# Another bound for half of the query weight and a new order of the opening, in a cross-attention and quantised feed-forward kernel on Trainium2

## What is computed

```python
def xattn(q, ctx, Wq, Wkv, Wout):           # 16 heads of 64; 1024 queries, 64 keys for each batch
    qp = q @ Wq.T                           # Wq 1024 x 1024
    k, v = split(ctx @ Wkv.T, 2)            # Wkv 2048 x 256
    scores = einsum(qh, kh) / sqrt(64)      # masked: query row i sees keys 0..i
    return (softmax(scores) @ vh) @ Wout.T  # Wout 1024 x 1024

def ffn(x, W):                              # per-tensor e4m3 quantisation of x and W
    return ((quant(x) @ quant(W).T) * (sx * sw)).astype(bfloat16)

x = x + xattn(layernorm(x), ctx, Wq, Wkv, Wout)
return x + ffn(layernorm(x), W)
```

## Time and profile before

| | before |
|---|---|
| median of 3 runs (lowest, highest) | 1737.17 us (1736.21, 1738.05) |
| profiled execution | 1736.76 us |
| its span, first to last instruction | 1734.8 us |
| TensorE busy | 1706.3 us (98%) |
| VectorE busy | 1337.4 us (77%) |
| ScalarE busy | 672.6 us (39%) |
| GpSimd busy | 182.7 us (11%) |
| mean granted TensorE clock | 0.999 of full speed |

### The profile page before, as it was taken

How to read it: one execution, slowest core, us unless ns; L and a number is a source line. 1 busy time by engine, 2 the same in 40 slices (tenths; PEclk the granted TensorE clock), 3 DMA queues, 4 the chain that set the end, 5 groups by cost and what they waited for, 6 DMA issues and landing times.

```text
span 1734.8 us, 27825 instructions
## 1 busy us (share of the span) xinstructions
PE 1706.3 (98%) x11485; PEld 810.6 (47%) x11513; DVE 1337.4 (77%) x1910; ACT 672.6 (39%) x638; POOL 182.7 (11%) x142
## 2 busy tenths in 40 slices
PE   7999999999999999999999999999999999999998
PEld 4544444445444544454445444544454444544444
DVE  8976687788866887788778877787778665877786
ACT  6632242223322332233223322332233222799985
POOL 0000000000000000000000000000000002255565
PEclk9999999999999999999999999999999999999999
DMA  9346645553545554545454545545554443799997
GB/s 351 105 112 161 152 97 119 136 147 87 128 121 134 109 125 114 139 107 126 121 128 122 114 130 131 112 104 125 133 125 111 97 86 71 264 314 323 324 250 217
DMA packets 387977, 258.95 MB, mean 149 GB/s; under 512 B 341920, under 2 KB 344480, under 8 KB 387616
## 3 DMA queue, kind: packets, MB, share of 16 engines
q1 hardware_dynamic: 387872, 257.47, 56.2%
HBM read 113.25 MB, written 67.11 MB: 104 GB/s over the span
## 4 chain that ended last, share of the span: by engine, by line
PE 84%; DVE 11%; ACT 3%; issue 1%; DMA 1%; SPq 0%; DVEq 0%; ACTq 0%
PE ps_all L730 34%; PE ps_all L746 32%; PE ps_all L903 12%; DVE m_buf L1271 3%; PE ps_all L713 3%; PE ps_all L683 1%; DVE n_buf L1265 1%; PE ps_all L755 1%; DVE tile_space L1340 1%; DVE hsum L1334 1%; DVE tile_space L1282 1%; DVE tile_space L1328 1%; PE ps_all L832 1%; DVE hmax L1323 1%; ACT n_buf L989 1%
## 5 line engine op out<-in xcount | busy, mean ns | idle before, releaser
L730 PE MATMUL ps_all<-m_buf,tile_space 128*128 128x504 f16 x3072 | 667.7, 376 | 0.6 <-DVE m_buf L1271 0.3
L746 PE MATMUL ps_all<-n_buf,tile_space 128*128 128x512 f16 x3024 | 667.4, 379 | 0.6 <-DMA tile_space<-tile_space 0.6
L730 PEld LDWEIGHTS ps_all<-m_buf,tile_space 128*128 128x128 f16 x3072 | 297.8, 98 | 351.9 <-issue 6.7
L746 PEld LDWEIGHTS ps_all<-n_buf,tile_space 128*128 128x128 f16 x3024 | 293.1, 98 | 356.6 <-issue 7.0
L575 POOL TENSOR_TENSOR rstd_x<-veps_x,minus_half 128x1 f32<-128x1 f32 x64 | 35.3, 551 | 1399.6 <-DVE veps_x L1295 1399.6
L1015 ACT ACTIVATE tile_space<-tile_space,neg_mean 128x1024 f32<-128x1024 f32 x56 | 64.3, 1149 | 278.1 <-DVE neg_mean L1360 278.1
L1011 ACT ACTIVATE tile_space<-tile_space,score_scale 128x1024 f32<-128x1024 f32 x64 | 73.4, 1147 | 233.2 <-DVE tile_space L1328 232.2
L1007 ACT ACTIVATE tile_space<-tile_space 128x1024 f16<-128x1024 f32 x64 | 67.6, 1057 | 190.5 <-DVE tile_space L1340 190.5
L1282 DVE SCALAR_TENSOR_TENSOR tile_space<-tile_space 128x1024 f16<-128x1024 f32 x64 | 78.4, 1225 | 70.7 <-ACT tile_space L1007 70.7
L1334 DVE TENSOR_REDUCE hsum<-tile_space 128x16 f32<-128x1024 f32 x64 | 77.9, 1217 | 58.3 <-ACT tile_space L1011 58.3
L1277 DVE SCALAR_TENSOR_TENSOR tile_space<-tile_space 128x1024 f16<-128x1024 f32 x64 | 78.3, 1223 | 52.8 <-ACT tile_space L1001 52.8
(11 more groups left out here) (170 smaller groups left out, 1566.9 us busy)
## 6 DMA issues: line engine op xcount, KB each, us to landing
tile_space<-in_x_dram SPq DMA_DIRECT2D x128, 512.0 KB, 4.0
x_scratch<-tile_space SPq DMA_DIRECT2D x56, 512.0 KB, 3.1
m_buf<-x_scratch SPq DMA_DIRECT2D x32, 512.0 KB, 5.6
out_dram<-m_buf SPq DMA_DIRECT2D x32, 512.0 KB, 4.3
tile_space<-x_scratch SPq DMA_DIRECT2D x24, 512.0 KB, 5.9
out_dram<-tile_space SPq DMA_DIRECT2D x24, 512.0 KB, 4.7
m_buf<-in_L_xattn_Wq_dram SPq DMA_DIRECT2D x4, 1024.0 KB, 11.9
n_buf<-in_L_xattn_Wout_dram SPq DMA_DIRECT2D x4, 1024.0 KB, 13.1
```

Of the source, the lines that this page charges most:

```text
L730: mm = nc.tensor.matmul(ps_s[:, half * HALF:half * HALF + RH], left[:, ls, c * P:(c + 1) * P], m_buf[:, rs, c, half * RH:(half + 1) * RH], ...
L746: mm = nc.tensor.matmul(to[:, cols], left[:, ls, j * P:(j + 1) * P], right[:, rs, j, cols], start=(c == 0 and i == 0), stop=(c == CT - 1 a ...
```

## The change

- **Query weight.** `wq_peak(0)` and `wq_peak(1)` go. ScalarE runs `wq_squares(0)` and `wq_squares(1)` instead: squares of a quarter, scaled by 2^-20 ahead of squaring, with the accumulator giving their sum for each partition (`wq_sum`). GpSimd, after its first power of the variance, waits for both and raises them to 0.5 (`wq_norm`); VectorE multiplies by 2^20. The norm of a row part bounds each of its elements, so the scale may be a smaller power of two than before. VectorE waits for `wq_norm` after `wq_peak(3)`. GpSimd has one constant more to set.
- **VectorE's order.** The centred context (L1501) moves ahead of the second sum of the key and value weight; `normalise(0, 0)` moves directly behind `variance(0, 0)`; `split_k_lo(0)` moves behind the query weight's spread; `split_v_lo(3)` moves behind `take_m(0, 0)`.
- **TensorE's order.** `expand(0)` no longer waits for the second copy of the transposed weight and stands ahead of `turn_peaks(0)`; `expand(5)` stands ahead of the wait for the last of these copies.
- **ScalarE's order.** `wq_squares(0)` ahead of `x_high(0, 0)`, `wq_squares(1)` behind `split_k_hi(0)`; `split_k_hi(2)` ahead of the two sums of the key and value weight; `copy_wkv(8, 3)` between the first two splits of the query weight. The output weight's sums 0 to 3 stood ahead of `copy_wkv(7, 2)` (0 and 1), ahead of the third scale (2) and between the value splits (3), sums 4 to 7 behind `take_m` 0 to 3. Now sums 0 and 1 stand between the value splits, sum 2 behind the last value split, and sums 3 to 7 behind `take_m` 1 to 5.

```diff
--- before.py
+++ after.py
@@ -123,7 +123,8 @@
...
         minus_half = sb("minus_half", [P, T], F32)
-        peaks = sb("peaks", [P, 10], F32)
+        peaks = sb("peaks", [P, 12], F32)
+        half = sb("half", [P, 2], F32)
         amax4_all = sb("amax4_all", [P, 4], F32)
...
@@ -175,6 +176,7 @@
...
         unread = [tile_space[:, i, :] for i in (12, 7)]
+        NORM_BY = 2.0 ** -20
         NG = 2 * NP
...
@@ -193,6 +195,8 @@
...
         wkv_sum = sem("wkv_sum")
+        wq_sum = sem("wq_sum")
+        wq_norm = sem("wq_norm")
         wout_hi = sem("wout_hi")
...
@@ -559,13 +563,14 @@
...
             nc.gpsimd.memset(minus_half[:], -0.5).then_inc(const_made, 1)
-            pool.wait_ge(const_made, 3)
+            nc.gpsimd.memset(half[:], 0.5).then_inc(const_made, 1)
+            pool.wait_ge(const_made, 4)
 
...
                                     pattern=[[-1, SK]], channel_multiplier=1).then_inc(const_made, 1)
-            pool.wait_ge(const_made, 5)
+            pool.wait_ge(const_made, 6)
             nc.gpsimd.tensor_copy(ident_bf[:], ident[:]).then_inc(const_made, 1)
...
@@ -574,7 +579,11 @@
...
 
-            with pool.Fori(0, T // 2) as j:
+            inverse_deviation(0, 0)
+            pool.wait_ge(wq_sum, 2)
+            nc.gpsimd.tensor_tensor(small[:, 4:6], peaks[:, 10:12], half[:], ALU.pow).then_inc(wq_norm, 1)
+            inverse_deviation(1, 1)
+            with pool.Fori(1, T // 2) as j:
                 inverse_deviation(2 * j, 0)
...
@@ -609,7 +618,7 @@
...
 
-            pe.wait_ge(const_made, 8)
+            pe.wait_ge(const_made, 9)
             pe.wait_ge(got_ctx, 16)
...
@@ -651,10 +660,12 @@
...
             turn_wkv(1)
+            pe.wait_ge(turned_read, 2)
+            expand(0)
             turn_peaks(0)
+            expand(1)
             pe.wait_ge(turned_read, 3)
-            for g2 in range(3):
-                expand(g2)
+            expand(2)
             pe.wait_ge(peak_read, 1)
...
@@ -665,8 +676,8 @@
...
             turn_peaks(2)
+            expand(5)
             pe.wait_ge(turned_read, 5)
-            expand(5)
             pe.wait_ge(peak_read, 3)
...
@@ -1091,37 +1102,50 @@
...
             copy_wkv(2, 1)
+
+            def wq_squares(i):
+                act.wait_ge(got_wq[i], 16)
+                if i == 1:
+                    act.wait_ge(wq_sum, 1)
+                nc.scalar.activation(tile_space[:, 7, :].bitcast(F16).rearrange("p (j c) -> p j c", c=H),
+                                     wq_f[:, 2 * i:2 * i + 2, :], ACT.Square, scale=NORM_BY,
+                                     accum_out=peaks[:, 10 + i:11 + i]).then_inc(wq_sum, 1)
+
+            wq_squares(0)
             x_high(0, 0)
...
             split_k_hi(0)
+            wq_squares(1)
             split_k_hi(1)
+            split_k_hi(2)
             act.wait_ge(got_wkv[2], 16)
             nc.scalar.activation(tile_space[:, 8, :], tile_space[:, 10, :], ACT.Abs, accum_out=peaks[:, 8:9]).then_inc(wkv_sum, 1)
-            split_k_hi(2)
             act.wait_ge(got_wkv[3], 16)
...
             split_k_hi(3)
-            sum_wout(0)
-            sum_wout(1)
             copy_wkv(7, 2)
+            act.wait_ge(scales_made, 2)
+            split_wq_hi(0)
             copy_wkv(8, 3)
-            act.wait_ge(scales_made, 2)
-            for i in range(3):
-                split_wq_hi(i)
-            sum_wout(2)
+            split_wq_hi(1)
+            split_wq_hi(2)
             act.wait_ge(scales_made, 3)
...
             split_v_hi(1)
-            sum_wout(3)
+            act.wait_ge(wq_sum, 2)
+            sum_wout(0)
             split_v_hi(2)
+            sum_wout(1)
+            take_m(0, 0)
             split_v_hi(3)
-            for c in range(4):
+            sum_wout(2)
+            for c in range(1, 6):
                 take_m(c, c // 2)
...
                     x_high(1, 1)
-                sum_wout(4 + c)
-            for c in range(4, CT):
+                sum_wout(2 + c)
+            for c in range(6, CT):
                 take_m(c, c // 2)
...
@@ -1493,27 +1517,27 @@
...
             wkv_sums(0)
-            wkv_sums(1)
-            then(nc.vector.tensor_reduce(small[:, 9:10], hmax[:, 0:8], AX.X, ALU.max))
-            spread_peaks(0, small[:, 8:10])
             dve.wait_ge(turned_read, 1)
...
                                     ALU.subtract).then_inc(ctx_made, 1)
+            wkv_sums(1)
+            then(nc.vector.tensor_reduce(small[:, 9:10], hmax[:, 0:8], AX.X, ALU.max))
+            spread_peaks(0, small[:, 8:10])
             variance(0, 0)
+            normalise(0, 0)
             all_peaks(0, small[:, 10:12])
...
             powers(slice(1, 2), 1, KV_TO / 2)
-            wq_peak(0)
-            normalise(0, 0)
-            wq_peak(1)
             x_low(0, 0)
             wq_peak(2)
-            split_k_lo(0)
             wq_peak(3)
+            dve.wait_ge(wq_norm, 1)
+            then(nc.vector.tensor_scalar(small[:, 4:6], small[:, 4:6], 1.0 / NORM_BY, None, ALU.mult))
             then(nc.vector.tensor_reduce(small[:, 13:14], small[:, 4:8], AX.X, ALU.max))
             spread_peaks(1, small[:, 13:14])
+            split_k_lo(0)
             split_k_lo(1)
...
@@ -1530,11 +1554,12 @@
...
             split_wq_lo(3)
-            for g2 in range(1, 4):
-                split_v_lo(g2)
+            split_v_lo(1)
+            split_v_lo(2)
             then(nc.vector.tensor_scalar(score_scale[:], from_f16[:, 0:1], from_f16[:, 1:2],
...
             take_m(0, 0)
+            split_v_lo(3)
             variance(1, 1)
...
```

## The result

| | before | changed |
|---|---|---|
| median, 20 runs each | 1736.37 us | 1739.43 us |
| lowest to highest | 1735.31 to 1738.27 | 1738.2 to 1740.6 |
| span of the profiled execution | 1734.8 | 1738.5 |

The changed kernel takes 1.0016 times the time of before, 95% interval 1.001 to 1.0022: slower, clear of no change, but not clear of the 0.2% that counts as none here. The medians differ by 3.06 us. The forecast was 1.7 us slower and 1738.9 us. The profiled execution lies at the slow end of the changed kernel's runs: their spans go from 1736.1 to 1738.5.

The account below looks back on a forecast made before the run. TensorE was taken to bound the kernel from 100 us on, so shifts in the opening arrive whole. 0.75 us (late sums) plus 1.0 (clock) gave 1.7 slower, from 1737.17 to 1738.9 us; range 1734.2 to 1740.9.

Parts of the forecast that it names:

- Parts 1 and 2: Opening: query weight norms and value weight between the splits bring the first key product from 46.51 to 42.5 us.
- The root's cover: GpSimd has the root of the norms at 18.9 us, covered by 2.8 us at VectorE's 21.7.
- Part 3: Output weight's last sum ends at 57.65 against 56.90; TensorE stands 4.1 us, first scores' chunk 4 starts 0.75 late.
- Part 4: TensorE's clock drops to half behind the 4.1 us standstill, costing 1.0 us (bounds 0 and 1.4).
- No drop at 30 us: TensorE's earlier half clock there was expected to vanish, its standstill shrinking to some 1.3 us.
- The remark that it would be hidden anyway: A clock drop at 30 us would not matter: TensorE's expansions are not what ends last at 42.3.
- (a): The opening's gain arrives because the sums are not last: 1734.0 us, perhaps 1733.2; chance 0.14.
- (b): Half clock behind the standstill holds over chunks 4 and 5 and both products: 3.7 us slower, 1740.9; chance 0.10.
- (c): In the opening the query weight or norms come 2 us late: 3.7 us slower, 1740.9; chance 0.04.
- (d): Squares cost ScalarE a second table load before the first exponential: 1739.2 us, 1740.6 by the skill; chance 0.06.

Follow-up runs that it names:

- filled: Changed kernel with useless matmuls filling both TensorE standstills, the output weight's first transposes moved into the second: 1736.58 against 1736.31 us before, ratio 1.0.
- only_sums: Kernel before with only the output weight's sums moved to where the change has them: 1742.10 against 1735.94 us, ratio 1.0035.
- short_sums: Changed kernel with each output weight sum reading 128 of 1024 columns: 1737.31 against 1736.31 us before, ratio 1.0007.
- max_back: Changed kernel without the norms, all four query weight quarters by maximum on VectorE: 1743.10 against 1736.31 us before, ratio 1.0039.
- both: Changed kernel with the sums early and the last value split back ahead of take_m(0): 1732.97 against 1735.94 us before, ratio 0.9982.
- v3_back: Changed kernel with the last value split back ahead of take_m(0), sums still late: 1737.94 us, ratio 1.0009 to before.
- both_max_back: The kernel of both without the norms, four maxima on VectorE: 1738.20 us, ratio 1.0009 to before.
- sums_early: Changed kernel with the output weight's sums moved earlier on ScalarE, the last behind take_m(3): 1734.46 against 1735.94 us before, ratio 0.9987.
- the two further looks: The changed kernel, unedited, profiled twice more: 1740.30 and 1740.47 us.

## Why the prediction was right, and where it was off

**Parts 1 and 2** held. Forecast for the second scales 25.7, the third 35.3, the first product 42.5; measured 25.6, 35.1 and 42.31. The anchor was the DMA of the last quarter, at 19.4: VectorE was released at 19.29. The root's cover held too.

**Part 3** held in mechanism and size. The forecast put chunk 4 0.75 us late at full clock; filled, where the clock is full, has it 0.77 late, take_m(3) on ScalarE at 50.81 (50.65) and the last sum read at 57.71 (57.65). In the changed kernel itself these came at 52.17 and 59.07, 1.4 to 1.5 us later than forecast, because the first drop stands ahead of them. VectorE's idle was 4.64 (4.8), TensorE's standstill 3.91 (4.1). only_sums shows that the sums' new place does it, short_sums that 2.7 us of the standstill are place and 1.2 us load.

**Part 4** is the step that fell short: the forecast allowed one drop at 1.0 us; there were two, of 1.6 and 1.8 in the profile. I named the wait for the moved value split as what sets the third product's start, and did not ask what TensorE does meanwhile: it stands 1.93 us, where it stood 1.26 with the split in its old place. Only the second standstill, longer than the one in the earlier trace rows, got a price. The size of the second drop was taken as chunk 4 and a part of one product; in the profile it covered chunk 4 and both products behind it (2.74 us against 1.57). With 0.77 + 1.6 + 1.0 to 1.8 the sum would have been 3.4 to 4.2; the three profiles of the changed kernel show 3.0 to 3.9 at tile 2 and 2.6 to 3.7 in span, and the medians 3.06.

**Luck.** As a difference the forecast missed 1.4 of 3.06 us; as a time it missed 0.5 (1738.9 against 1739.43). The time came out closer because the forecast was counted from 1737.17, the median of three runs, and the median of twenty is 1736.37. The forecast's own range, 1737.9 to 1740.0, means 0.7 to 2.8 us slower than the median it was counted from: the time lies in it, the difference just above it.

No drop at 30 us was forecast, and none came (1.00). The remark that it would be hidden anyway was wrong: in it lie the value weight's transposes, which ScalarE's copies wait for. only_sums, with no drop there, has its first product 0.8 us earlier than the kernel before, and in max_back the drop costs 0.9.

**The rivals.** (a), the early gain arrives, didn't happen in the changed kernel, but the kernel of **both** shows that it was there to be had, 3.0 us. (b) happened in part: the second drop lasted over chunk 4 and both products in one profile. Its total of 3.7 us came nearer to the 3.06 measured than the forecast's 1.7, but by one long drop and not by two. (c) didn't happen. (d) didn't: one table load, at 0.74. The Trainium skill's list of functions in every set ("ScalarE: Activation LUTs", "Table sets: the hidden batching unit") leaves squares out, but here squares, copies, absolute values and exponentials ran under one load of 1.28 us.

## What to carry to other kernels

When work is moved later on an engine that has slack on the whole, look for the one wait that counts all of it, and ask what stands behind that wait on the waiting engine: here one transpose of TensorE, and all its work behind that, stood behind eight small sums. A bound gained early is kept only if everything else that the next common step waits for comes as early. And price the standstills that a new order makes on TensorE, not only the waits: each of them can be paid twice, the second time in clock.

## What the runs showed of the hardware

- The clock fell to half in the six profiles with a standstill of 3.91 us, and in short_sums after 2.72 us. After 1.26 to 1.28 us it stayed full in the profiles of the kernel before, v3_back, both, both_max_back and only_sums.
- After a standstill of 1.93 us it fell in four profiles (the changed kernel three times, sums_early) and stayed full in two (short_sums, max_back), with the same order of work before it. What decides is open: the two further looks were meant to show it changing within one kernel, and didn't; the spans of sums_early and short_sums, in two groups each, suggest that it does.
- Near 26 us TensorE stands still twice, with one transpose of 0.3 to 0.5 us between. After 1.77 and 0.90 us the clock fell (kernel before, 0.50 from 28.9 us), after 3.24 and 0.81 (max_back) and 3.89 and 0.95 (both_max_back) too; after 1.23 and 0.89 (only_sums) it stayed full.
- Transposes are slowed as well: 16 of them took 1.94 us at full clock, 3.65 where the clock was 0.50.
- A power on GpSimd over two columns took 0.71 us, over one 0.55 to 0.57.
